# A feed-forward layer with two experts for each token: the product per pair of batches in four 64x64 tiles

## What is computed

```python
W = weights[condition]                       # 64 of 16 matrices [64, 64]
y = einsum('bct,bcd->bdt', x, W)             # one 64x64 product per batch
logits = y @ W_gate + b_gate                 # 8 experts
_, top_idx = top_k(logits, 2)
y_all = relu(einsum('bsd,edh->bseh', y, W_e) + b_e)
out = x + take_along_axis(y_all, top_idx[..., None], axis=2).mean(axis=2)
```

## Time and profile before

| | |
|---|---|
| median of 3 runs | 899.07 us (899.04 to 900.41) |
| the profiled execution | 897.66 us |
| its span in the trace | 896.0 us |
| PE busy | 850.3 us (95%) |
| DVE, ACT, POOL busy | 408.5, 255.8, 513.4 us |
| matmuls of line 509 (the product), 128 records | 63.5 us |
| matmuls of line 573 (the body) | 343.3, 341.1 and 340.9 us in three groups that overlap; 76% of the chain that ended last |
| DMA, mean over the span | 182 GB/s |

### The profile page before, as it was taken

The page is one execution under the profiler, slowest core; times in us unless marked ns, Lnnn a source line. Parts: engine busy times, 40 slices in busy tenths (PEclk is TensorE's granted clock), DMA queues, the critical chain, the costliest instruction groups (busy, mean ns, idle before and its releaser), DMA issues.

```text
span 896.0 us, 16403 instructions
## 1 busy us (share of the span) xinstructions
PE 850.3 (95%) x4102; PEld 675.5 (75%) x4103; DVE 408.5 (46%) x537; ACT 255.8 (29%) x309; POOL 513.4 (57%) x560
## 2 busy tenths in 40 slices
PE   6899799996999999999999999999999999999992
PEld 3454478885878888888888888888888888888882
DVE  3788756426733373335533373336433733333320
ACT  4565411105511151123321241115211511222210
POOL 2177777647567666654675557555655565555311
PEclk9999999998999999999999999999999999999997
DMA  9999999678965586545854495546664664444433
GB/s 322 416 414 394 391 330 326 177 205 240 304 162 126 108 251 158 113 100 135 249 113 94 94 281 117 103 100 207 175 117 94 187 119 101 96 98 96 78 48 47
DMA packets 54472, 163.23 MB, mean 182 GB/s; under 512 B 14378, under 2 KB 14986, under 8 KB 54442
## 3 DMA queue, kind: packets, MB, share of 16 engines
q0 software_dynamic: 26720, 77.79, 39.6%
q1 hardware_dynamic: 21306, 67.65, 20.9%
q10 hardware_dynamic: 6416, 17.44, 5.0%
HBM read 106.47 MB, written 70.94 MB: 198 GB/s over the span
## 4 chain that ended last, share of the span: by engine, by line
PE 80%; DMA 6%; DVE 5%; issue 4%; POOL 3%; ACT 1%; ACTq 0%; POOLq 0%; DVEq 0%; SPq 0%
PE psO L573 76%; PE psO L509 3%; POOL rows L416 2%; DMA rows<-in_x 1%; DMA out<-rows,first_to 1%; DMA wgc<-wgc 1%; PE psG L521 1%; DVE turned L814 1%; DMA out<-ys,first_to 1%; DMA out<-rows,idx_s 1%; POOL out L430 0%; DMA raw<-in_L_cond_weights 0%; DVE w_lo L827 0%; DMA rows<-y_rows,idx_g 0%; POOL idx_g L412 0%
## 5 line engine op out<-in xcount | busy, mean ns | idle before, releaser
L573 PE MATMUL psO<-w_hi,a_hi 128*128 (+1 forms) x1104 | 343.3, 392 | 11.7 <-DVE a_lo L962 8.8
L573 PE MATMUL psO<-w_lo,a_hi 128*128 (+1 forms) x1104 | 341.1, 390 | 0.0
L573 PE MATMUL psO<-w_hi,a_lo 128*128 (+1 forms) x1104 | 340.9, 390 | 0.0
L416 POOL DMA_INDIRECT rows<-y_rows,idx_g x248 | 256.0, 1032 | 108.0 <-issue 52.7
L573 PEld LDWEIGHTS psO<-w_hi,a_hi 128*128 128x128 f32 x1104 | 207.4, 189 | 55.9 <-issue 11.0
L573 PEld LDWEIGHTS psO<-w_lo,a_hi 128*128 128x128 f32 x1104 | 208.3, 189 | 43.5
L573 PEld LDWEIGHTS psO<-w_hi,a_lo 128*128 128x128 f32 x1104 | 207.9, 188 | 43.2
L962 DVE TENSOR_TENSOR a_lo<-ys,a_hi 128x1024 fp32r<-128x1024 f32 x62 | 75.9, 1224 | 112.7 <-ACT a_hi L700 112.7
L688 ACT ACTIVATE ys<-ys 128x1024 f32<-128x1024 f32 x33 | 35.0, 1061 | 263.0 <-DVE ys L924 263.0
L688 ACT ACTIVATE rows<-rows 128x1024 f32<-128x1024 f32 x33 | 35.0, 1061 | 252.2 <-DVE rows L924 252.2
L924 DVE TENSOR_TENSOR rows<-psO,bias 128x1024 f32<-128x1024 f32 x33 | 40.3, 1222 | 127.8 <-PE psO L573 112.4
(11 more groups left out here) (126 smaller groups left out, 328.4 us busy)
## 6 DMA issues: line engine op xcount, KB each, us to landing
raw<-in_L_ffn_W_e SPq DMA_DIRECT2D x56, 512.0 KB, 6.3
rows<-in_x SPq DMA_DIRECT2D x32, 512.0 KB, 8.8
y_rows<-ys ACTq DMA_DIRECT2D x32, 512.0 KB, 8.8
out<-in_x SPq DMA_DIRECT2D x14, 1024.0 KB, 6.8
bias<-in_L_ffn_b_e SPq DMA_DIRECT2D x8, 512.0 KB
rows<-y_rows,idx_g POOLq DMA_INDIRECT x248, 2.9
raw<-in_L_ffn_W_e POOLq DMA_DIRECT2D x4, 512.0 KB, 8.9
bias<-in_L_ffn_W_e POOLq DMA_DIRECT2D x4, 512.0 KB, 8.8
```

The costliest lines, as they stand in the source:

```text
L416: pool.indirect_dma_start(out=rows[:, slot, a * DQ:(a + 1) * DQ], out_offset=None, in_=y_parts, in_offset=bass.IndirectOffsetOnAxis(ap=idx ...
L573: last = nc.tensor.matmul(ps[:, h * BANK:(h + 1) * BANK], a[:, p, k * P:(k + 1) * P], w[:, bass.ds(slot + (k * H + h * BANK), BANK)], star ...
```

## The change

The product is made of four matmuls with weights of 64x64, in four tiles of the array: rows 0 to 63 of the array take the first batch of the pair and rows 64 to 127 the second; columns 0 to 63 take the first half of the features and columns 64 to 127 the second. Each matmul has 512 columns. The result has other partitions than before: the half of the features `f` and the output channel `d` are in the partitions (`f * 64 + d`), and the batch `i` and the 512 features of the half are in the columns, so batch `i` is in one bank of PSUM. `bd` is now 64 columns wide, and its zeroes are gone with the memset.

The store of `ys` becomes two, one for each half `f`: 64 partitions, and from each partition two pieces of 2 KB (one for each batch). The semaphore of a buffer counts 32 where it counted 16.

The gate has 16 matmuls of 256 columns where it had 32 of 128, `wgb` is half as large, and the copy to `LT` has 256 columns where it had 128. `unstack` has one more matmul: the bias first, then one for each batch.

```diff
-                    for h in range(D // BANK):
-                        last = nc.tensor.matmul(psO[n % 2][:, h * BANK:(h + 1) * BANK], bd[:, s, :],
-                                                rows[:, s, h * BANK:(h + 1) * BANK], start=True, stop=True)
+                    for f in range(2):
+                        for i in range(PAIR):
+                            at = slice(i * C, (i + 1) * C)
+                            last = nc.tensor.matmul(
+                                psO[n % 2][f * C:(f + 1) * C, i * BANK:(i + 1) * BANK], bd[at, s, :],
+                                rows[at, s, :].rearrange("p (k q j) -> p q k j", k=KD, q=Q)[:, 2 * f:2 * f + 2, :, :],
+                                start=True, stop=True, tile_position=(i * C, f * C), skip_group_check=True)
                     last.then_inc(s_y, 1)
...
-                    for b in range(half * (NB // 2), (half + 1) * (NB // 2)):
+                    both = turned[:, g % 2, :, :].rearrange("p (i b) t -> p b i t", i=PAIR)
+                    for b in range(half * (NB // 4), (half + 1) * (NB // 4)):
                         j = b % Q
-                        last = nc.tensor.matmul(psG[j * R:(j + 1) * R, 0:P], wgb[:, b, :], turned[:, g % 2, b, :],
-                                                start=(b < Q), stop=(b >= NB - Q), skip_group_check=True,
+                        last = nc.tensor.matmul(psG[j * R:(j + 1) * R, 0:PAIR * P].rearrange("p (i t) -> p i t", i=PAIR),
+                                                wgb[:, b, :], both[:, b, :, :],
+                                                start=(b < Q), stop=(b >= NB // 2 - Q), skip_group_check=True,
                                                 tile_position=(0, j * R))
...
-                    nc.tensor.matmul(psR[:, sums_at], LT[:, :], stack[:, :], start=True, stop=False)
-                    nc.tensor.matmul(psR[:, sums_at], ones_f[0:1, :], gb, start=False, stop=True).then_inc(s_u, 1)
+                    nc.tensor.matmul(psR[:, sums_at], ones_f[0:1, :], gb, start=True, stop=False, skip_group_check=True)
+                    for i in range(PAIR):
+                        last = nc.tensor.matmul(psR[:, sums_at.start + i * PAIR * E:sums_at.start + (i + 1) * PAIR * E],
+                                                LT[:, i * P:(i + 1) * P], stack[:, 0:PAIR * E], start=False, stop=True,
+                                                skip_group_check=True)
+                    last.then_inc(s_u, 1)
...
-                    nc.scalar.copy(ys[:, s, :].rearrange("p (q k j) -> p q k j", q=Q, k=KD),
-                                   psO[n % 2][:, :].rearrange("p (k q j) -> p q k j", q=Q, k=KD)).then_inc(s_yc, 1)
+                    nc.scalar.copy(ys[:, s, :], psO[n % 2][:, :]).then_inc(s_yc, 1)
                     act.wait_ge(s_yc, n + 1)
-                    act.dma_start(y_dram[P + n * P:P + (n + 1) * P, :], ys[:, s, :]).then_inc(s_yout[s], 16)
+                    for f in range(2):
+                        act.dma_start(y_dram[P + n * P:P + (n + 1) * P, f * BANK:(f + 1) * BANK]
+                                      .rearrange("(i d) c -> d i c", i=PAIR),
+                                      ys[f * C:(f + 1) * C, s, :].rearrange("d (i c) -> d i c", i=PAIR)
+                                      ).then_inc(s_yout[s], 16)
...
-                    nc.scalar.copy(LT[:, :], psG[:, 0:P]).then_inc(s_LT, 1)
+                    nc.scalar.copy(LT[:, :], psG[:, 0:PAIR * P]).then_inc(s_LT, 1)
...
-                V.memset(bd, 0.0).then_inc(s_bd0, 1)
```

More of the change, by code:

```diff
@@ L55, in build @@
     LAND = 16 * 2 * G
+    YW = 2 * 16
     RAW = 4
@@ L88, in build @@
             lend("w_lo_0", [P, 2 * HALF])
-            wgb = lend("wgb", [P, NB, R])
+            wgb = lend("wgb", [P, NB // 2, R])
             wgc = lend("wgc", [P, NB, E])
-            LT = lend("LT", [P, P])
+            LT = lend("LT", [P, PAIR * P])
             ident = lend("ident", [P, P])
@@ L130, in build @@
         cw = raw[:, 3, :].rearrange("p (n c) -> p n c", n=NCOND)
-        bd = raw[:, 2, 0:G * P].rearrange("p (g c) -> p g c", g=G)
+        bd = raw[:, 2, 0:G * C].rearrange("p (g c) -> p g c", g=G)
         ones_f = raw[:, 2, G * P:G * P + P]
@@ L398, in early @@
                     for s in range(G):
-                        pool.wait_ge(s_yout[s], 16 * (t + 1))
+                        pool.wait_ge(s_yout[s], YW * (t + 1))
                     pool.wait_ge(s_from, t + 1)
@@ L644, in _ @@
                 act.wait_ge(s_cw, 16 * (PAIR + 1))
-                act.wait_ge(s_bd0, 2)
                 regs = [act.alloc_register(f"cond{i}") for i in range(G * PAIR)]
@@ L654, in diagonal @@
                         at = slice(C * i, C * (i + 1))
-                        nc.scalar.copy(bd[at, s, C * i:C * (i + 1)],
+                        nc.scalar.copy(bd[at, s, :],
                                        cw[at, bass.ds(c, 1), :].rearrange("p o c -> p (o c)")).then_inc(s_bd, 1)
@@ L661, in y_out @@
                     if n >= G:
-                        act.wait_ge(s_yout[s], n // G * 16)
+                        act.wait_ge(s_yout[s], n // G * YW)
                         act.wait_ge(s_turn, n - G + 1)
-                    nc.scalar.copy(ys[:, s, :].rearrange("p (q k j) -> p q k j", q=Q, k=KD),
-                                   psO[n % 2][:, :].rearrange("p (k q j) -> p q k j", q=Q, k=KD)).then_inc(s_yc, 1)
+                    nc.scalar.copy(ys[:, s, :], psO[n % 2][:, :]).then_inc(s_yc, 1)
                     act.wait_ge(s_yc, n + 1)
-                    act.dma_start(y_dram[P + n * P:P + (n + 1) * P, :], ys[:, s, :]).then_inc(s_yout[s], 16)
+                    for f in range(2):
[3 more added lines that the diff above has]
+                                      ).then_inc(s_yout[s], 16)
                 def logits_out(g):
@@ L732, in _ @@
                     act.wait_ge(s_sc[g], LAND)
-                act.wait_ge(s_yout[0], 16 * NG)
+                act.wait_ge(s_yout[0], YW * NG)
                 act.wait_ge(s_turn, NTILE)
@@ L821, in gate_blocks @@
                         at = slice(a * R, (a + 1) * R)
-                        own(V.tensor_copy(wgb[at, :, a * E:(a + 1) * E], wgc[at, :, :]))
+                        f, dh = a // 2, a % 2
+                        own(V.tensor_copy(wgb[at, :, dh * E:(dh + 1) * E],
+                                          wgc[at, f * (NB // 2):(f + 1) * (NB // 2), :]))
                     dve.sem_inc(s_wg, 1)
@@ L930, in finish_early @@
                     elif t >= FIRST:
-                        dve.wait_ge(s_yout[t % OS], 16 * NG)
+                        dve.wait_ge(s_yout[t % OS], YW * NG)
                     finish(tile(0, t), 0)
@@ L1019, in _ @@
                 dve.sem_inc(s_idx, 1)
-                dve.wait_ge(s_yout[1], 16 * NG)
+                dve.wait_ge(s_yout[1], YW * NG)
                 for q in range(Q):
```

## The result

| | before | after |
|---|---|---|
| median of 4 runs | 899.39 us (899.04 to 900.41) | 916.77 us (915.82 to 918.01) |
| ratio, 95% interval | | 1.0192 (1.0174 to 1.0210) |
| profiled execution, span | 897.66, 896.0 us | 916.77, 915.1 us |
| body's first matmul | 109.95 us | 128.66 us |
| end of PE's long wait | 211.91 us | 231.41 us |

The changed kernel is 17.4 us slower. The prediction was 898.3 us, in a range from 893.5 to 904.5, so the time lies outside it, on the side where the prediction had put a rival at 908.

The account below looks back on a forecast made before the run. The prediction took full DMA engines to bound most of the front, then a DVE chain from 68.84 us. Its terms, -2.6 + 0.75 + 0.1 + 1.0 = -0.75 us, took 899.07 to 898.3 us, range 893.5 to 904.5.

Parts of the forecast that it names:

- Second store on ACT: In the front, 27 added issues of 0.326 us, 9 us, fit into ACT's 20.3 us of waits; cost nothing.
- 57 of the 70 us: From 24 to 94 us, ACT's busy 41.44 us plus 23 old and 23 new issues of 0.33 us.
- DMA decides: Likeliest case, chance 0.47: DMA engines set the front's pace, the end loop gives a little; 896.1 to 901 us.
- -2.6 us from three products: Three shorter products before `choose` at the front's end save 0.74 + 0.93 + 0.93 us, limited by DVE's idle time.
- The product's own saving: On PE, each product falls from 1.98 to 1.05 us, saving 0.93 us.
- +0.25: The third matmul of `unstack` adds 0.25 us each time, three times on the chain: 0.75 us.
- Pieces of 2 KB, +1.0: Smaller store pieces in the front cost the DMA engines 1.0 us; low bound zero, high bound 4.6 us.
- The clock falls: Rival, chance 0.08: gaps on PE drop its clock to 1.2 GHz, slowing gate, `unstack` and `ranks`; 903.6 us.
- The stores in halves are slow: Rival: 64-partition stores slow the front's DMA; strong form +9 us, 908, chance 0.12; mild form 902, chance 0.12.
- a rate under 390 GB/s: Sign in the profile after that the stores cost; landing times of y over 10 us were the alternative sign.
- The tiles don't run together: Rival, chance 0.04: a product takes 2.0 us, 901 us in all, or 3.9 us, +45 us.
- The whole -0.75 arrives: The 0.75 us gained at the body's start carries through the gathers and the long wait to the end.

Follow-up runs that it names:

- e5: The changed kernel with the old y store, one per tile of 128 partitions and 4 KB rows (`out` wrong, timing only); 900.30 us against 899.12 before.
- e8: e5 with eight small bf16 matmuls behind each product, into a bank nobody reads, to keep PE busy; 900.36 us against 899.12 before.
- e2: The kernel before with its one y store of 128 partitions cut into 2 KB pieces (`out` wrong, timing only); 902.97 us, ratio 1.0031.
- e3: The kernel before with each y store as two of 64 partitions, rows of 4 KB, issued by ACT; 914.0 us, ratio 1.0147.
- e6: The kernel before with each y store as two of 64 partitions, rows of 4 KB, issued by SP; 904.85 us, ratio 1.0066.
- e1: The changed kernel with both half stores issued by SP instead of ACT; 906.48 us against 900.46 before, ratio 1.0066.
- e7: The kernel before with its one y store per tile issued by SP instead of ACT; 903.67 us, ratio 1.0039.
- e11: The kernel before with each y store as two of 128 partitions and 512 columns, issued by ACT; 908.72 us, ratio 1.0107.
- e10: The changed kernel with the first half store issued by ACT and the second by SP; 910.29 us against 899.55 before, ratio 1.0122.

## Why the prediction was wrong

- **The step that failed: "Second store on ACT", "I cost it at nothing".** I priced the new issues at 0.326 us, the duration of one issue of another shape with nothing in front of it. The pair took 1.24 us, and up to 4.41. The text even had the test: "If that room goes [...] ACT becomes the engine that turns last", and found 57 of the 70 us. With the pair at 1.24 us the same sum is 41.44 + 23 x 1.24 = 70.0 of 70 us, with nothing left for the gaps between instructions; the runs showed ACT as the engine that turns last, with 30% of the chain in its issues. The stretched pairs from 109 us on came on top. The cost of an issue in a new shape was in no row, and I gave it no bounds. In hindsight, a bound of twice the known duration would have put the case "ACT turns last" among the rivals.
- **The mechanism "DMA decides" held only while ACT had room.** It held in e5 and e8 (401 and 409 GB/s, no gain from a shorter product). In after ACT took 2.95 us for a tile at the least and 3.62 on average, for 3.01 before, and the rate fell to 347.
- **-2.6 us from three products: not collected.** e5 gained 0.13 us in the last loop. The product's own saving was right (1.09 us for 1.05), `unstack` was right (+0.29 for +0.25), `share` at the half clock was in the rival on the clock only. What the loop would give at full clock without e8's filler was not run; by subtraction it is some 0.4 us for the last of the three.
- **Pieces of 2 KB, +1.0: too low.** e2 measured +4.7 us at the body's start and +2.5 us in the median, near the high bound of 4.6. In after little of it adds to ACT's loop: its body starts 1.9 us behind that of e3, which has pieces of 4 KB, and the longer pairs of issues are part of that.
- **The rival "The clock falls":** it fell, to 0.77, as the rival said, and at the lower level the product takes 1.99 us and a half gate 1.93 in e5. But its time of 903.6 was too high: e5 has that clock and 900.30 us. (The sum's 2.6 us for products were not there to be lost.)
- **The rival "The stores in halves are slow", 908:** the right side, the wrong place. It blamed the store's side in the DMA engines; e6 cleared them for halves with rows of 4 KB, e1 for the halves of after but for some 2 us, and e3 put it on the issue. That its 908 lies nearest is luck. Its sign, a rate under 390 GB/s, came true for another reason.
- **"The tiles don't run together": they do**, eight records in 1.09 us.
- **"The whole -0.75 arrives" was right as a path:** the shift of the front reaches the end, 18.7 us at the body's start, 19.5 at the end of the long wait, 19.1 in the span.

The Trainium skill, page DMA: Bandwidth & Descriptors, section Issuing engines are not separate DMA queues, says that starting transfers on several engines saves only sequencer time, "which is usually small relative to the DMA itself". By transfer that holds here, 0.63 us beside a landing time of 6.6 us; but the engine that issues pays it for each tile, and the pair is 1.24 of the 2.95 us in ACT's shortest period. The same page of the Trainium skill, section Rules for kernel authors, advises against two transfers for two halves of the partitions, since both run on the same DMA engines. The runs agree that they gain nothing (e6 904.85, e7 903.67 us); e3 shows that on a busy issuing engine they also cost, 13.5 us.

## What to carry to other kernels

Count a DMA issue as work of the engine that issues it, with a duration from a row of the same shape and the same place in a row of issues; where no such row exists, bound it from twice the known one upwards (here 0.33 us became 0.63 in the median) and ask how much room that engine has in each period. When a transfer is split or its issue is moved, look at what stands behind it on that engine: here the next copy out of PSUM on ACT, and the index loads of the body on SP. A share of DMA time near 1 doesn't say that the DMA engines decide: look at the rate and the landing times beside it. And a shorter matmul was worth nothing in a stretch where another engine or the DMA rate set the period: measure it with the rest of the change taken away.

## What the runs showed of the hardware

- **An issue's duration depends on the transfer's shape and on what is issued ahead of it.** On ACT, the median for a y store of 512 KB: 0.326 us (one, 128 partitions, 4 KB), 0.366 (one, pieces of 2 KB). For two transfers of 256 KB: 0.88 us for both (128 partitions, 2 KB), 1.11 (64 partitions, 4 KB), 1.25 (64 partitions, two pieces). SP took as long, 0.61 us for each half with two pieces (e1) and 0.60 with rows of 4 KB (e6), and 0.326 for the whole store (e7).
- **It stretches.** From 109 to 126 us pairs in after took 1.93, 2.22, 3.22 and 4.41 us, in e3 1.67 to 3.99, in e11 up to 2.0; a single issue for each tile stayed at 0.32 to 0.43 on ACT in before, e2 and e5, and one half store for each tile (e10) reached 1.04. Single issues on SP stretched too, to 1.66 us in e1, 1.96 in e6 and 0.92 in e7. In that stretch SP issues the stores and the large copies to `out`, but e11 has a pair of 1.77 us at 82.70, ahead of them. Whether full queues, the number of pieces or SP's issues do it was not tried and stays open.
- **Four tiles of 64x64 run together:** eight float32 records of 512 columns in 1.09 us, where four records on the whole array took 1.98. At the lower level of the clock the eight took up to 1.99 (e5).
- **A lower clock of TensorE cost little** where the DMA rate set the pace: a granted clock of 0.77 from 24 to 94 us (e5) gave 900.30 us, against 899.12 before at 0.98, and 900.36 with a filler that held it at 0.95 (e8).
